# One unit of chunked linear attention: three tiled TensorE stretches put into one, headed by the key transposes, with ScalarE's order refitted

## The chip, the cores and the metric

The kernel is one program on one core of a Trainium2 chip. The metric is the device time of one execution in microseconds. Engines are called PE (TensorE), DVE (VectorE), ACT (ScalarE), POOL (GpSimd) and SP (SyncE, which issues the DMAs).

## The reference, cut to what matters

A small hybrid model on 2 x 1024 tokens of 256 features: linear attention with decay (32 heads of 64), an FFN, softmax attention (16 heads of 16), and the FFN again, each behind a layer norm and with a residual. The change touches the linear attention alone:

```python
qkv = silu(h @ qkv_w.T); q, k, v = split(qkv)          # 32 heads of 64
def step(state, blk):                                  # blocks of the sequence
    aw    = einsum("bhid,bhjd->bhij", qi, ki) * dd     # scores with decay mask
    intra = einsum("bhij,bhjd->bhid", aw, vi)
    inter = einsum("bhid,bhde->bhie", qi * qd_, state)
    new   = state * bd_ + einsum("bhsd,bhse->bhde", ki * kd_, vi)
    return new, intra + inter
attn = rmsnorm(attn) * norm_w;  gate = sigmoid(h @ gate_w.T)
x = x + (gate * attn) @ out_w.T
```

## The kernel before, in words

`linear_attention` walks the work in 32 units. A unit is four heads (two pairs, `pr`) on 512 tokens; unit `u` is `unit(i, j)` with `u = 8 i + j`. Four units make one quad of heads (2048 tokens), whose weights (`w_quads`, 1280 KB) SP loads behind the unit with `j % 4 == 3` of the quad before. The sequence is cut into chunks of 64 tokens, eight in a unit.

PE has two kinds of work in a unit. The **dense** kind uses the whole 128x128 array: `project(..., "v")`, `"g"` (gate), `"k"`, `"q"` and `outputs` (the out projection), each in two halves `n` on the PSUM banks `R[0]` and `R[1]`, each half 12 matmuls (of 256 columns for v and the out projection, of 512 for g, k and q). The **tiled** kind uses the array as quarters of 64x64: `carried` (q times the state, 64 matmuls, 56 where the unit starts a sequence), `within` (masked scores times v, 32 for the blocks of one parity, 32 for the other), `scores` (64) and `state_sums` (k times v per chunk, 64). `turned_keys` transposes the keys by 16 transposes of 64 rows x 128 columns.

The order on PE in a unit j before (lines 716 to 766):

- `carried(j)`, `within(j, True)`, first half of `scores(j+2)` (tiled)
- v of j+2 (dense)
- `within(j, False)`, `state_sums(j+1)`, second half of `scores(j+2)` (tiled)
- g of j+1, k of j+3 (dense)
- `turned_keys(j+2)` (64x128 transposes)
- `outputs(j)`, q of j+3 (dense)

Each engine has its own order written out by hand, with semaphores between them. ACT evicts each projection from `R[n]` through an activation (`evict`, `silu_ok`; a projection into `R[n]` waits until its last content is read), rounds y to its high part (`yh`), squares the outputs (`sq`) and writes the transposed keys times their decay (`keys`: four activations, `kd_ok`, which `state_sums` waits for). DVE forms y = gate times output (`gated`), runs the chain of states (`states`), masks the scores (`masks`) and adds the out projection to the sum (`sums`), then splits weights. POOL decays the queries (`decayed`, after `half_ok`), writes the low part of y, adds the squares and writes the low parts of weights. Units 16 to 27 also carry a piece `c` of the FFN's weight quantisation (`quant`) on ACT, DVE, POOL and SP.

In the last two units (`last`, j = 6 and 7) there is no v, k or q left; ahead of unit 30 PE sums the squares (`fin.squares`, 16 matmuls), and ACT takes a square root of them at the head of its unit 30.

Of the kernel before, what the change touches and what calls it, by code (L numbers as in the profile page):

```python
# [167 lines left out]
def linear_attention(nc, ctx, X, ident, ident_in, hTh, hTl, hidden, w_quads, c_quads, ln2, fin, q, WF, w_ffn, q_ffn, small):  # L168

    with ExitStack() as mem:  # L170
# [41 lines left out]
        def step(i, j):  # L212
            return (i + 1, j - 8) if j >= 8 else (i, j)

        def has(last, j, ahead):
            return not (last and j + ahead > 7)
# [10 lines left out]
        def links(i, j):  # L227
            i, j = step(i, j)
            return LINKS[8] * i + LINKS[j + 1]
# [112 lines left out]
        def _(act):  # L342
            def evict(i, j, kind, n, count):
                act.wait_ge(proj_ok, count + 1)
                bank = R[n][:]
                if kind == "v":
                    act.activation(v[:, j % 4, 2 * n:2 * n + 2, :], bank.rearrange("p (t n) -> p t n", t=2),  # L347
                                   ACT.Silu).then_inc(silu_ok, 1)
                elif kind == "g":
                    act.activation(g[:, j % 2, n, :], bank, ACT.Tanh, scale=0.5).then_inc(silu_ok, 1)  # L350
                elif kind == "k":
                    act.activation(k[:, j % 2, n, :], bank, ACT.Silu).then_inc(silu_ok, 1)
                else:
                    act.activation(q[:, j % 4, n, :], bank, ACT.Silu).then_inc(silu_ok, 1)  # L354
# [13 lines left out]
            def unit(i, j, last, c=None):  # L368
                n0 = evicted(i, j, last)
                if last and j == 6:  # L370
                    act.wait_ge(init_ok, 4)
                    act.wait_ge(fin.ss_ok, 1)
                    act.activation(fin.std[:, 0:4], SC[0][:, 0:4], ACT.Sqrt, bias=fin.epst[:],
                                   scale=4.0 / FEAT).then_inc(fin.std_ok, 1)
                zh, _ = high_low(last, j)
                if has(last, j, 2):
                    for n in range(2):
                        evict(*step(i, j + 2), "v", n, n0 + n)
                    n0 = n0 + 2
                for pr in range(2):  # L380
                    act.wait_ge(y_ok, 16 * i + 2 * j + pr + 1)
                    act.activation(zh[:, pr, :], y[:, pr, :], ACT.Copy).then_inc(yh_ok, 1)  # L382
                if last and j == 7:
                    ln2["scaled"](act, 0, hbuf)
                for pr in range(2):
                    act.wait_ge(sqa_ok, 16 * i + 2 * j + pr + 1)
                    act.activation(sq[:, pr, :], O[pr][:], ACT.Square).then_inc(sq_ok, 1)
                    if has(last, j, 1) and not (last and j == 6):
                        evict(*step(i, j + 1), "g", pr, n0 + pr)
                if last and j == 6:  # L390
                    for pr in range(2):
                        evict(i, 7, "g", pr, n0 + pr)
                if has(last, j, 1):
                    n0 = n0 + 2
                if has(last, j, 3):
                    for n in range(2):
                        evict(*step(i, j + 3), "k", n, n0 + n)
                if has(last, j, 2):
                    for pr in range(2):
                        keys(*step(i, j + 2), pr)  # L400
                if c is not None:
                    quant.rounding(act, c)
                if has(last, j, 3):
                    for n in range(2):
                        evict(*step(i, j + 3), "q", n, n0 + 2 + n)
                if c is not None:
                    quant.overflow(act, c)
                if last and j == 6:
                    act.activation(fin.std[:, 4:8], SC[0][:, 4:8], ACT.Sqrt, bias=fin.epst[:],
                                   scale=4.0 / FEAT).then_inc(fin.std_ok, 1)  # L410
                    ln2["deviation"](act, 0)
                if last and j == 7:
                    ln2["high"](act, 0, banks=SC)
# [39 lines left out]
            for n in range(2):  # L453
                evict(0, 0, "g", n, 12 + n)
            for pr in range(2):
                keys(0, 1, pr)
                evict(0, 2, "k", pr, 14 + pr)
            for n in range(2):
                evict(0, 2, "q", n, 16 + n)
# [132 lines left out]
        def _(pe):  # L592
# [49 lines left out]
                                             k[half[h], j % 2, pr, c * P:(c + 1) * P], ident[half[h], half[h]])  # L642
                m.then_inc(kb_ok, 1)

            def scores(j, pairs=range(2)):
                for pr in pairs:
                    for c in range(GC):
                        for h in range(2):
                            for par in range(2):
                                tok = slice((2 * c + par) * CH, (2 * c + par + 1) * CH)  # L650
                                at = (pr * GC + c) * CH
                                m = pe.matmul(SC[h][half[par], at:at + CH], k[half[h], j % 2, pr, tok],
                                              q[half[h], j % 4, pr, tok], start=True, stop=True)
                if 1 in pairs:
                    m.then_inc(sc_ok, 1)

            def state_sums(j):
                for pr in range(2):
# [10 lines left out]
            def carried(j):  # L669
                n0 = 1 if j % 2 == 0 else 0  # L670
                for n in range(n0, 2 * GC):
                    tok = slice(n * CH, (n + 1) * CH)
                    at = 8 * (j % 2) + n - 1
                    for pr in range(2):
                        for h in range(2):
                            pe.matmul(O[pr][half[h ^ pr], tok], S[half[h], at, pr, :], qd[half[h], pr, tok],
                                      start=n == n0, stop=False, skip_group_check=True)
# [38 lines left out]
            def unit(i, j, last):  # L716
                n0 = evicted(i, j, last)
                pe.wait_ge(mask_ok, 16 * i + 2 * j + 2)
                pe.wait_ge(s_link, links(i, j))
                pe.wait_ge(qd_ok, 16 * i + 2 * j + 2)  # L720
                pe.wait_ge(sq_ok, 16 * i + 2 * j + 1)
                carried(j)
                within(j, True).then_inc(half_ok, 1)
                if has(last, j, 2):
                    pe.wait_ge(silu_ok, n0 - 1)
                    pe.wait_ge(mask_ok, 16 * i + 2 * j + 4)
                    scores((j + 2) % 8, (0,))
                if has(last, j, 2):
                    for n in range(2):
                        pe.wait_ge(silu_ok, n0 + n - 1)  # L730
                        project(*step(i, j + 2), "v", n)
                    n0 = n0 + 2
                pe.wait_ge(half_ok, 8 * i + j + 1)
                within(j, False).then_inc(o_ok, 1)
                if last and j == 7:
                    outputs(i, 6, last, evicted(i, 6, last) + 2)
                    pe.wait_ge(mask_ok, 8 * NQ)
                    pe.wait_ge(fin.std_ok, 2)
                    ln2["turn"](pe, 0, H=hbuf, banks=SC)
                if has(last, j, 1):  # L740
                    pe.wait_ge(kd_ok, 32 * i + 4 * j + 8)
                    state_sums((j + 1) % 8)
                if has(last, j, 2):
                    scores((j + 2) % 8, (1,))
                if has(last, j, 1):
                    for n in range(2):
                        if has(last, j, 2):
                            pe.wait_ge(silu_ok, n0 + n - 1)
                        else:
                            pe.wait_ge(acc_ok, 16 * i + 2 * j + n)  # L750
                        project(*step(i, j + 1), "g", n)
                    n0 = n0 + 2
                if has(last, j, 3):
                    for n in range(2):
                        pe.wait_ge(silu_ok, n0 + n - 1)
                        project(*step(i, j + 3), "k", n)
                    n0 = n0 + 2
                if has(last, j, 2):
                    pe.wait_ge(s_link, links(i, j + 1))
                    turned_keys((j + 2) % 8)  # L760
                if not (last and j == 6):
                    outputs(i, j, last, n0)
                if has(last, j, 3):
                    for n in range(2):
                        pe.wait_ge(acc_ok, 16 * i + 2 * j + n + 2)
                        project(*step(i, j + 3), "q", n)
# [30 lines left out]
            for n in range(2):  # L797
                pe.wait_ge(silu_ok, 11 + n)
                project(0, 0, "g", n)
            pe.wait_ge(s_link, links(0, 0))  # L800
            turned_keys(1)
            for n in range(4):
                pe.wait_ge(silu_ok, 13 + n)
                project(0, 2, "kq"[n // 2], n % 2)
# [1294 lines left out]
```

## Time and profile before

| | |
|---|---|
| median of 3 runs | 1116.5 us (1115.07 to 1119.46) |
| profiled execution, its own time | 1122.47 us |
| span of the profiled execution | 1120.7 us |
| PE busy | 1074.7 us (96%) |
| DVE, ACT, POOL busy | 594.9, 620.4, 495.6 us |
| linear attention loop, first to last unit | from 50.9 to about 640 us |
| one unit | 19.25 us, 19.15 where it starts a sequence |

In the timeline a row is a group of like instructions: start, time from the first start to the last end, engine, line, what is written and read, how many; in square brackets the idle time before it. Matmuls overlap, so two rows that follow each other overlap too; the time a matmul takes from the next is the distance of their starts. In `--windows` rows there follow PE, PE's weight loads, DVE, ACT and POOL busy with their counts, the granted clock as a share, and the DMA share.

### The profile page before, as it was taken

Reading aid. Unit: us, or ns where it says so; the run is one execution under the profiler, and the core shown is the slowest. Engines: PE = TensorE matmul, PEld = TensorE weight load, DVE = VectorE, ACT = ScalarE, POOL = GpSimd, SP = SyncE. Lnnn points to the kernel's source line nnn. Section 1 sums busy time; section 2 is a strip of 40 time slices with the busy share of each in tenths; the row PEclk is TensorE's granted clock in tenths of the full one; section 3 lists DMA queues with packets and bytes.
Section 4 is the critical chain, followed back from the end, with each engine's and each line's share of the span. In section 5 each row is a group of like instructions: output and inputs, shape, how many; then the busy total and the mean of one; then the engine's idle time right before and its main releaser. Section 6 shows DMA issues by size and latency. Waiting matters only on the chain. (4 is left out here: it accounts for less than half of the span.)

```text
span 1120.7 us, 33656 instructions
## 1 busy us (share of the span) xinstructions
PE 1074.7 (96%) x14448; PEld 832.7 (74%) x14448; DVE 594.9 (53%) x1341; ACT 620.4 (55%) x1172; POOL 495.6 (44%) x528
## 2 busy tenths in 40 slices
PE   4999999999999999999999899978899999999998
PEld 4888888888888888888888788856444444445787
DVE  6143434333343545454453755587777778775433
ACT  4553444444443555555554575585477777766663
POOL 2354445354454555554644537644233332221346
PEclk9999999999999999999999989988999999999999
DMA  3100101001001002002004110057523233000001
GB/s 132 56 3 3 56 3 50 9 3 49 17 2 49 25 23 77 24 16 84 17 23 155 35 53 1 18 123 173 100 58 58 58 58 59 2 3 1 1 20 57
DMA packets 19296, 49.15 MB, mean 44 GB/s; under 512 B 2576, under 2 KB 13648, under 8 KB 16464
## 3 DMA queue, kind: packets, MB, share of 16 engines
q1 hardware_dynamic: 19152, 47.04, 15.4%
q8 instruction: 114, 1.87, 0.7%
q14 instruction: 30, 0.25, 0.1%
HBM read 36.08 MB, written 10.75 MB: 42 GB/s over the span
## 5 line engine op out<-in xcount | busy, mean ns | idle before, releaser
L1884 DVE TENSOR_REDUCE aa_mx<-aa_S 128x1 f32<-128x640 f32 (+1 forms) x192 | 174.3, 953 | 54.5 <-PE aa_S L1597 52.6
L506 DVE SCALAR_TENSOR_TENSOR la_y<-la_g,la_O 128x512 f32<-128x512 f32 x64 | 41.1, 683 | 222.5 <-PE la_O L686 222.5
L1789 ACT ACTIVATE aa_PT<-keep 128x512 f32<-128x512 f32 (+1 forms) x204 | 111.6, 580 | 47.1 <-PE keep L1623 45.0
L596 PE MATMUL la_R<-a_hTh,WF 128*128 128x512 f32 x384 | 130.2, 404 | 4.4 <-DVE a_hTl L153 4.4
L1508 POOL TENSOR_SCALAR_AFFINE_SELECT aa_PT<-aa_PT 128x256 f32<-128x256 f32 (+1 forms) x112 | 49.2, 440 | 184.4 <-ACT aa_PT L1789 181.1
L304 POOL TENSOR_TENSOR la_yl<-la_y,la_yh 128x512 fp32r<-128x512 f32 x62 | 79.1, 1299 | 90.2 <-ACT la_yh L382 90.2
L291 POOL TENSOR_TENSOR la_qd<-q,la_C 128x512 f32<-128x512 f32 x64 | 80.8, 1284 | 80.0 <-PE la_O L686 79.7
L513 DVE TENSOR_TENSOR X<-la_R,X 128x512 f32<-128x512 f32 x64 | 44.2, 691 | 118.4 <-PE la_R L596 118.3
L1594 PE MATMUL aa_S<-aa_stacks 96*128 96x512 bf16 (+3 forms) x384 | 99.1, 331 | 4.4 <-DVE aa_mx L1884 3.9
L347 ACT ACTIVATE la_v<-la_R 128x512 f32<-128x512 f32 x64 | 38.2, 598 | 113.5 <-PE la_R L596 113.5
L1069 POOL TENSOR_TENSOR f_fl<-f_f,f_fh 128x512 fp32r<-128x512 f32 x48 | 61.8, 1296 | 66.4 <-ACT f_fh L932 66.4
L354 ACT ACTIVATE q<-la_R 128x512 f32<-128x512 f32 x64 | 38.3, 598 | 93.6 <-PE la_R L596 93.6
L312 POOL TENSOR_TENSOR fin_sqacc<-fin_sqacc,la_sq 128x512 f32<-128x512 f32 x64 | 86.1, 1346 | 7.7 <-DVE X L1191 3.1
L596 PEld LDWEIGHTS la_R<-a_hTh,WF 128*128 128x128 f32 x384 | 72.8, 190 | 22.1 <-DVE a_hTl L153 4.8
L495 DVE SCALAR_TENSOR_TENSOR la_S<-la_S,la_C,la_Y 128x64 f32<-128x64 f32 x448 | 88.6, 273 | 0.2
L596 PE MATMUL la_R<-a_hTh,la_Wh 128*128 128x512 f32 x192 | 77.6, 404 | 0.0
L596 PE MATMUL la_R<-a_hTl,WF 128*128 128x512 f32 x192 | 76.2, 397 | 0.0
L596 PE MATMUL la_R<-a_hTh,la_Wl 128*128 128x512 f32 x192 | 75.9, 396 | 0.0
L596 PE MATMUL la_R<-a_hTl,la_Wh 128*128 128x512 f32 x192 | 75.8, 395 | 0.0
L1623 PE MATMUL keep<-aa_stacks 99*128 99x512 bf16 (+3 forms) x260 | 72.0, 326 | 2.3 <-DMA aa_stacks<-aa_MXT 0.8
L1789 ACT ACTIVATE aa_PT<-aa_ST 128x512 f32<-128x512 f32 (+1 forms) x100 | 58.3, 583 | 25.4 <-PE aa_ST L1623 24.4
L1639 PE MATMUL aa_OB<-aa_PT,aa_V 128*32 128x512 f32 (+3 forms) x768 | 71.7, 492 | 0.0
(306 smaller groups left out, 2804.3 us busy)
## 6 DMA issues: line engine op xcount, KB each, us to landing
la_Wraw<-w_quads_dram SPq DMA_DIRECT2D x7, 1280.0 KB, 6.8
aa_stacks<-k_parts SPq DMA_DIRECT2D x16, 256.0 KB, 6.8
q_parts<-aa_QP SPq DMA_DIRECT2D x8, 384.0 KB, 4.7
aa_stacks<-q_parts SPq DMA_DIRECT2D x8, 384.0 KB, 4.6
k_parts<-aa_KP SPq DMA_DIRECT2D x8, 384.0 KB, 4.9
qw_w<-w_ffn_dram SPq DMA_DIRECT2D x12, 192.0 KB, 2.4
q_ffn<-qw_w SPq DMA_DIRECT2D x12, 192.0 KB, 1.9
X<-hidden_dram SPq DMA_DIRECT2D x4, 512.0 KB, 7.3
```

The source lines that it names most:

```text
L291: pool.tensor_tensor(qd[:, pr, :].rearrange("p (c t) -> p c t", t=CH), q[:, j % 4, pr, :].rearrange("p (c t) -> p c t", t=CH), C[:, slot, ...
L304: pool.tensor_tensor(zl[:, pr, :], y[:, pr, :], zh[:, pr, :].bitcast(F32), ALU.subtract).then_inc(yl_ok, 1)
L312: pool.tensor_tensor(sqacc[:, tok], sqacc[:, tok], sq[:, pr, :], ALU.add).then_inc(sqa_ok, 1)
L495: ins = dve.scalar_tensor_tensor(S[:, at, pr, :], S[:, at - 1, pr, :], C[:, slot, C_B + pr:C_B + pr + 1], U, ALU.mult, ALU.add)
L596: m = pe.matmul(out, a, b, start=n == 0, stop=n == len(pairs) - 1)
L1069: pool.tensor_tensor(fl[:, tb % 2, it, :], f[:, n % FR, :], fh[:, tb % 2, it, :].bitcast(F32), ALU.subtract).then_inc(fl_ok, 1)
L1508: pool.affine_select(part, part, [[0, max(nh, 2)], [1, P]], ALU.is_ge, 0.0, base=0, channel_multiplier=-1).then_inc(cut_ok, 1)
L1594: ins = pe.matmul(bank[:, col:col + k1 - k0], Q[0:SROWS, j, qt * P:(qt + 1) * P], K[0:SROWS, j, k0:k1], start=True, stop=True)
L1623: ins = pe.matmul(ST[at % NB][:, e * w:(e + 1) * w], KS[g % NSL][0:KROWS, h + e, kt * P:(kt + 1) * P], QS[g % NSL][0:KROWS, h + e, q0:q0 + ...
L1639: ins = pe.matmul(OB[32 * j:32 * j + 32, q0 - qb * TB:q0 - qb * TB + w], V[:, 8 * (g // NG) + kt, HG * (g % NG) + j, :], PT[:, (NM2 * g + ...
L1789: act.activation(PT[:, (NM2 * g + b) % NPT, h:h + nh, 0:w], ST[at % NB][:, 0:nh * w].rearrange("p (h q) -> p h q", h=nh), ACT.Exp, scale=S ...
L1884: dve.reduce_max(out, src, AXX).then_inc(s1_free, 1)
```

## The change

PE's order in a unit becomes: `turned_keys(j+1)`, `carried(j)`, `within(j, True)`, all of `scores(j+2)`, `within(j, False)`, `state_sums(j+1)`; then the dense v (j+2), g (j+1), k (j+3), `outputs(j)`, q (j+3). The transposes are made for the keys of j+1 at the head of unit j, where before they were made for j+2 at its end; the prologue's transposes of unit 1 go with them. ACT writes the keys of j+1 first in its unit, then yh, then the squares each followed by an eviction of v, then g, k, q. The other engines' programs are as before.

```diff
 # ACT
-                if has(last, j, 2):
-                    for n in range(2):
-                        evict(*step(i, j + 2), "v", n, n0 + n)
-                    n0 = n0 + 2
+                if has(last, j, 1):
+                    for pr in range(2):
+                        keys(*step(i, j + 1), pr)
                 for pr in range(2):
                     act.wait_ge(y_ok, 16 * i + 2 * j + pr + 1)
                     act.activation(zh[:, pr, :], y[:, pr, :], ACT.Copy).then_inc(yh_ok, 1)
+                values = 2 if has(last, j, 2) else 0
...
                     act.activation(sq[:, pr, :], O[pr][:], ACT.Square).then_inc(sq_ok, 1)
-                    if has(last, j, 1) and not (last and j == 6):
+                    if values:
+                        evict(*step(i, j + 2), "v", pr, n0 + pr)
+                n0 = n0 + values
+                if has(last, j, 1) and not (last and j == 6):
+                    for pr in range(2):
                         evict(*step(i, j + 1), "g", pr, n0 + pr)
...
-                if has(last, j, 2):
-                    for pr in range(2):
-                        keys(*step(i, j + 2), pr)
...
             for pr in range(2):
-                keys(0, 1, pr)
                 evict(0, 2, "k", pr, 14 + pr)
 # PE
+                if has(last, j, 1):
+                    turned_keys((j + 1) % 8)
                 carried(j)
                 within(j, True).then_inc(half_ok, 1)
                 if has(last, j, 2):
-                    pe.wait_ge(silu_ok, n0 - 1)
+                    pe.wait_ge(silu_ok, n0)
                     pe.wait_ge(mask_ok, 16 * i + 2 * j + 4)
-                    scores((j + 2) % 8, (0,))
-                if has(last, j, 2):
-                    for n in range(2):
-                        pe.wait_ge(silu_ok, n0 + n - 1)
-                        project(*step(i, j + 2), "v", n)
-                    n0 = n0 + 2
+                    scores((j + 2) % 8)
                 pe.wait_ge(half_ok, 8 * i + j + 1)
                 within(j, False).then_inc(o_ok, 1)
...
                     state_sums((j + 1) % 8)
                 if has(last, j, 2):
-                    scores((j + 2) % 8, (1,))
+                    for n in range(2):
+                        pe.wait_ge(silu_ok, n0 + n - 1)
+                        project(*step(i, j + 2), "v", n)
+                    n0 = n0 + 2
...
-                if has(last, j, 2):
-                    pe.wait_ge(s_link, links(i, j + 1))
-                    turned_keys((j + 2) % 8)
                 if not (last and j == 6):
                     outputs(i, j, last, n0)
...
-            pe.wait_ge(s_link, links(0, 0))
-            turned_keys(1)
```

## Rows read from the trace of the kernel before

**Rows 1.** The page: busy time, share of the span and instructions of PE.
```profile
PE 1074.7 (96%) x14448; PEld 832.7 (74%) x14448; DVE 594.9 (53%) x1341; ACT 620.4 (55%) x1172; POOL 495.6 (44%) x528
```

**Rows 2.** Busy time of the engines in two whole units, 13 and 14.
```profile
319.72:338.87 19.15, 19.15 (x350) 16.62 (x349) 7.50 (x23) 8.56 (x16) 9.61 (x8) 1.00 0.01 2
300.47:319.72 19.25, 19.25 (x358) 16.72 (x357) 7.48 (x24) 8.55 (x16) 10.28 (x9) 1.00 0.01 3
```

**Rows 3.** Timeline of PE in unit 13, around the projection of v.
```profile
301.45 0.65 PE L686 MATMUL la_O<-la_A,la_v 64*64 64x64 f32 x32
301.92 0.65 PE L652 MATMUL la_SC<-q,la_k 64*64 64x64 f32 x32
302.50 0.39 PE L596 MATMUL la_R<-la_Wh,a_hTh 128*128 128x256 f32 x1
302.72 0.28 PE L596 MATMUL la_R<-la_Wl,a_hTh 128*128 128x256 f32 x1
...
305.30 0.28 PE L596 MATMUL la_R<-la_Wh,a_hTl 128*128 128x256 f32 x1
305.51 0.69 PE L686 MATMUL la_O<-la_A,la_v 64*64 64x64 f32 x32
306.02 1.11 PE L663 MATMUL la_Y<-la_v,la_kd 64*64 64x64 f32 x64
```

**Rows 4.** Timeline of PE in unit 13, around the transposes; one row cuts them at eight.
```profile
312.77 0.39 PE L596 MATMUL la_R<-a_hTl,WF 128*128 128x512 f32 x1
313.00 0.40 PE L596 MATMUL la_R<-a_hTh,WF 128*128 128x512 f32 x1
313.33 0.71 PE L641 MATMUL la_Y<-ident,la_k 64*128 64x64 f32 x16
...
313.33 0.47 PE L641 MATMUL la_Y<-ident,la_k 64*128 64x64 f32 x8
...
313.98 0.38 PE L596 MATMUL la_R<-la_Wh,la_yh 128*128 128x256 f32 x1
314.20 0.29 PE L596 MATMUL la_R<-la_Wl,la_yh 128*128 128x256 f32 x1
```

**Rows 5.** Timeline of DVE in unit 13: y.
```profile
306.37 1.28 DVE L506 SCALAR_TENSOR_TENSOR la_y<-la_g,la_O 128x512 f32<-128x512 f32 x2 [7.30 <-PE la_O L686]
```

**Rows 6.** Timeline of ACT in unit 13 and at the head of unit 14.
```profile
307.09 1.23 ACT L382 ACTIVATE la_yh<-la_y 128x512 fp32r<-128x512 f32 x2 [0.88 <-DVE la_y L506]
308.22 0.58 ACT L387 ACTIVATE la_sq<-la_O 128x512 f32<-128x512 f32 x1
...
312.04 0.60 ACT L352 ACTIVATE la_k<-la_R 128x512 f32<-128x512 f32 x1 [0.80 <-PE la_R L596]
...
314.08 1.57 ACT L365 ACTIVATE la_kd<-la_Y,la_C 128x256 f32<-128x256 f32 x4
...
319.83 0.60 ACT L354 ACTIVATE q<-la_R 128x512 f32<-128x512 f32 x1 [0.80 <-PE la_R L596]
```

**Rows 7.** Timeline of POOL in unit 13: the decayed queries.
```profile
302.21 2.52 POOL L291 TENSOR_TENSOR la_qd<-q,la_C 128x512 f32<-128x512 f32 x2 [0.70 <-PE la_O L686]
```

**Rows 8.** Timeline of ACT at the head of unit 18, a unit with quantisation.
```profile
397.51 0.52 ACT L1159 ACTIVATE qw_k<-qw_w 128x384 f32<-128x384 f32 x1
```

**Rows 9.** Timelines of PE and of ACT at units 30 and 31.
```profile
623.43 1.04 PE L676 MATMUL la_O<-la_qd,la_S 64*64 64x64 f32 x56
...
629.86 1.16 PE L676 MATMUL la_O<-la_qd,la_S 64*64 64x64 f32 x64 [0.21 <-issue]
...
623.58 1.28 ACT L373 ACT_TABLE_LOAD   x1 [3.09 <-PE la_SC L1180]
```

**Rows 10.** Unit 15: PE's scores, SP's weight load; the page's row of instruction loads.
```profile
345.35 1.06 PE L652 MATMUL la_SC<-q,la_k 64*64 64x64 f32 x32
...
344.70 0.33 SPq L253 DMA_DIRECT2D la_Wraw<-w_quads_dram  x1
...
q8 instruction: 114, 1.87, 0.7%
```

More of the change, by code:

```diff
@@ L643, in turned_keys, with scores @@
                 m.then_inc(kb_ok, 1)
-            def scores(j, pairs=range(2)):
-                for pr in pairs:
+            def scores(j):
+                for pr in range(2):
                     for c in range(GC):
@@ L653, in scores @@
                                               q[half[h], j % 4, pr, tok], start=True, stop=True)
-                if 1 in pairs:
-                    m.then_inc(sc_ok, 1)
+                m.then_inc(sc_ok, 1)
             def state_sums(j):
```

## The prediction

> **What bounds the kernel now.** I read the page's busy times first, then the engines' busy time in windows of whole units, then the timeline of PE instruction by instruction, and last the timelines of ACT, DVE and POOL beside it. PE is busy 96% of the span [rows 1], and in a unit of the linear attention it is never idle: 19.15 of 19.15 us and 19.25 of 19.25 us, at a granted clock of 1.00, which is the level of 2.4 GHz [rows 2]. The other engines are busy 7.5 to 10.3 us of the 19 in the same windows. So in this stage, some 590 of 1120.7 us, nothing but the time from one matmul's start to the next's counts, and a wait would have to be new to matter. Busy, though, hides something: a busy PE is not a PE at its pitch. The timeline shows it at each change between whole-array matmuls and tiled ones. A dense matmul of 256 columns starts (305.30 - 302.72) / 22 = 0.117 us after the one before, one of 512 columns 0.23 us (313.00 - 312.77), and 32 tiled matmuls of an undisturbed run take 0.47 us (301.45 to 301.92) [rows 3, 4]. At the changes the steps are longer, and the change is about those.
>
> **The change part by part.** No instruction is added or removed, on any engine. PE's matmuls of a unit are the same in number and shape. What changes is how often PE passes between dense and tiled: three rounds (into tiled and back) in a unit before, one after.
>
> *The round around v goes.* From the rows [rows 3]: the 32 scores ahead of v take 0.58 us until the first dense matmul, 0.11 over 0.47. The first dense one takes 0.22 until the second, 0.10 over 0.117. The last dense one takes 0.21 until `within`, 0.09 over 0.117. The first 32 tiled ones behind it take 0.51, 0.04 over 0.47. Sum 0.34 us. It goes in the 30 units that have a projection of v: 10.2 us.
>
> *The round around the transposes goes.* The last dense matmul takes 0.33 us until the transposes, 0.10 over 0.23. The eighth transpose ends 0.47 us after the first's start, the sixteenth 0.71 [rows 4]: the last four pairs take 0.24 us, 0.06 a pair, where the first three steps take 0.25 for 0.18, so 0.06 over. (With the 0.22 us that one lasts, the last pair starts at 313.82.) From there to the dense one at 313.98 it is 0.16, 0.10 over a pair, and that first dense one takes 0.22, 0.10 over. Sum about 0.35; I take 0.34. It goes in 30 units and once in the prologue: 31 x 0.34 = 10.5 us.
>
> *A new junction comes.* The transposes (64 rows x 128 columns) now stand straight ahead of `carried` (64x64), 31 times. No row of before shows these two side by side. Below: `within`, `state_sums` and `scores` follow each other at the usual pitch though they differ in operands and banks, so 0; nothing in it could make it a gain. Above: as much as a whole round, 0.34. I take 0.15, the nearest rows' price for leaving one array shape (0.10 to 0.11) and for the first group in the new one (0.04 to 0.06), without the 0.10 that only the full-width first weights cost. 31 x 0.15 = 4.7 us. The rule that bears on it is in the Trainium skill, "TensorEngine Tiling (Array Packing)", Key Properties: a change of the tiling mode drains the array, a change of the tile does not. The trace agrees where it can: 64x64 work on other quarters of the array flows at pitch, and each of six mode changes costs. By that rule 64x128 to 64x64 is a change of mode and is paid, against this change; by the reading that both count as tiled the sum would be 4.7 us better.
>
> *Waits, one by one, with T the start of a unit's transposes.* The times follow from the pitches above: transposes to T+0.55, junction, `carried` T+0.7 to 1.6, `within` to 2.1, `scores` to 3.05, `within` to 3.5, `state_sums` to 4.45, then v0 from 4.6, v1 6.05, g0 7.45, then one half each 1.4 us, `outputs` from 13.1, q to 18.65.
> (a) `state_sums` waits for the keys, which before were written half a unit early. ACT first finishes the last eviction of q, 0.11 to 0.71 us into the unit by where it lies before (319.83 against 319.72) [rows 6]. The transposes are out at T+0.75, the four key activations take 1.57 us [rows 6], so they end at T+2.4, with the 0.52 us of quantisation ahead of them [rows 8] at T+2.7. PE wants them at T+3.5: 0.8 us of slack. Behind the keys on ACT stands yh, which can't start before T+4.6 anyway.
> (b) `scores` now waits for both halves of q, evicted at T+0.7; wanted at T+2.1.
> (c) g0 waits for the eviction of v0, which now stands behind yh and a square. y starts 0.35 us after the last `within` matmul is issued (306.37) [rows 5] or so, T+3.9; yh0 0.72 us later, the square 1.13 after that (307.09, 308.22), so it runs from T+5.75 to 6.3 [rows 6]. v0's last matmul ends at T+6.25. The eviction thus runs at T+6.3 to 6.9, and g0 wants the bank at T+7.45: 0.5 us of slack, as much as k has behind g before, where ACT idles 0.80 us ahead of an eviction [rows 6] and PE does not wait. Behind it: the second square, v1, g0, each ahead of its need.
> (d) POOL's decayed queries start at T+2.3 in place of T+1.7 and take 2.52 us [rows 7]; wanted at T+18.65. The wait of `within(j, False)` for the first half is covered by the scores between them. `outputs` and `sums` keep their distance to the unit's end, so POOL's, DVE's and SP's later work does too. The state chain follows y at T+5.2 and has the whole dense stretch.
>
> *The end.* In unit 30 ACT has a table load of 1.28 us [rows 9] and a root (0.3 allowed) ahead of the keys, so they end 0.15 + 1.28 + 0.3 + 1.57 = 3.3 us after the squares; PE would reach `state_sums` after 2.8. Behind the sums the chain of states on DVE releases unit 31. Before it starts 6.43 us behind unit 30 (629.86 against 623.43) [rows 9], just about when the states are ready; I find 7.35 from the transposes on where the transposes and junction alone give 7.1. Loss 0.3 us.
>
> *Sum.* -10.2 - 10.5 + 4.7 + 0.3 = -15.7 us. A unit goes from 19.25 to 18.7 us. The span goes from 1120.7 to 1105.0 and the profiled execution's own time from 1122.5 to 1106.8. The median of the runs shown is 6.0 under that execution, so 1116.5 - 15.7 = 1100.8.
>
> **The rivals.**
> *A. PE's instructions don't keep up.* The longest tiled run now is 16 + 64 + 64 + 64 + 64 = 272 matmuls with as many weight loads, before it was 128. The instruction queue loaded 114 blocks, 1.87 MB, so 16 KB each [rows 10], and PE's 2 x 14448 instructions [rows 1] over 114 make 253 a block. A tiled run eats a block in 127 x 0.0146 = 1.9 us, and one long run now eats two. For it: in unit 15 the 32 scores at the very end of a run took 1.06 us in place of 0.65 [rows 10], 0.4 us lost, in the stretch that SP's weight load began at 344.70. Against: it is one of 30 units. If each long run lost that 0.4, the gain would be 15.7 - 12 = 4 us: 1113. In a sentence for itself: the Trainium skill, "Runtime: NRT & Kernel Launch", Instruction fetch mechanics, gives PE room for 2048 instructions in blocks of 256, by which a run of 544 would never wait; no run here shows that room.
> *B. The same, with the weights in the way (slower than before).* SP starts a load of 1280 KB in seven units at `o_ok`, now T+3.9, with `state_sums` and v behind it. If PE then stood until its next block came through behind that load, it would wait up to the load's length, some 5 us: 7 x 5 = 35, less 15.7, gives 1136. It makes the kernel slower from 2.2 us a load on. Against: v and g eat only some 70 instructions in their 2.8 us, and in unit 15 it cost 0.4.
> *C. ACT is late for v.* If y, yh and square came 1.1 us later than reckoned, PE would stand 0.6 us ahead of g0 in 30 units: the gain is spent, 1117. From 0.5 us of lateness on it costs something. Nothing ahead of y on DVE is in its way: it idled 7.30 us there [rows 5].
> *D. The junction costs a whole round.* Then 31 x 0.19 more: 1107.
>
> **How the numbers follow.** My forecast (with a junction anywhere from 0 to D) has 0.80: 1096 to 1107. A 0.09, B 0.04, C 0.07. The range that should hold it 8 times in 10 reaches from the junction at 0 to a little past D, towards A: 1095 to 1110. A measurement here tells 0.5%, 5.6 us, from no change. Faster by more: the 0.80 and half of A and a little of C, 0.86. Within: the rest of A and most of C, 0.09. Slower: B and the tail of C, 0.05.
>
> **What would show it.** A unit of 18.7 us (18.6 at a sequence's start) with PE busy throughout; two dense-to-tiled steps fewer; behind the transposes a first step of `carried` between 0.06 and 0.4 us, which is the junction; no row of PE waiting for ACT's keys or for v's eviction; ACT's idle time ahead of v0's eviction near 0. Wrong would be a unit above 19.0, a step over 0.3 us inside a tiled run (A, B), or a gap ahead of g0 (C).

## The result, and the profile after

The changed kernel takes 1142.1 us (median of 4 runs, 1141.32 to 1145.1) where the kernel before takes 1116.3 beside it: a ratio of 1.021, 95% interval 1.018 to 1.024, so 25.8 us slower by the medians where 15.7 us faster was forecast. (A slip ahead of the prediction: a half of g, k or q is 6 matmuls of 512 columns, not 12; the durations used there, 1.4 us a half, are those of 6.)

The busy times of the page, to be read against [rows 1], and the waits of PE in the whole span (line waited at, releaser, us in all, times, longest):

```profile
PE 1060.5 (93%) x14445; PEld 830.8 (73%) x14448; DVE 591.1 (52%) x1341; ACT 619.7 (54%) x1172; POOL 493.5 (43%) x528
```

```profile
PE la_Y L662 <- issue: 19.3, 15, 1.7
...
PE la_O L685 <- issue: 8.2, 8, 1.5
...
PE la_SC L652 <- issue: 3.7, 5, 1.4
...
PE la_R L596 <- issue: 1.7, 3, 0.7
...
PE la_Y L662 <- ACT la_kd L365: 0.3, 1, 0.3
```

"issue" is idle time for which no semaphore and no DMA of the program can be named. There are 31 such waits, 32.9 us in all, where the loop before had next to none; one wait of 0.3 us is for ACT's keys. Two whole units (13 and 14), and the loop from the first `carried` to the last one's start, before and after (after the window: PE, PE's weight loads, DVE, ACT, POOL busy, granted clock, DMA share, GB/s):

```profile
310.90:331.37 20.47, 19.03 (x360) 16.83 (x357) 7.57 (x24) 8.56 (x17) 10.23 (x9) 1.00 0.01 2
331.37:351.54 20.17, 18.88 (x352) 16.71 (x349) 7.59 (x23) 8.56 (x17) 9.27 (x8) 1.00 0.01 2
51.31:655.70 604.39, 571.07 (x10753) 505.50 (x10749) 242.19 (x725) 279.70 (x537) 289.00 (x224) 1.00 0.10 33
```

```profile
50.94:629.86 578.92, 578.47 (x10749) 502.72 (x10749) 245.69 (x725) 279.52 (x532) 291.22 (x224) 1.00 0.10 34
```

The units answer to [rows 2]: 20.5 and 20.2 us for 19.25 and 19.15. The loop took 25.5 us more, at the same granted clock of 1.00 and with 7 us less of PE busy: the whole difference of the medians is here. (The profiled spans differ by 19.6 only, since the profile of before had the lower clock level, 1.2 GHz, for longer behind this loop: the mean granted clock over the span is 0.989 against 0.997.)

PE's timeline in unit 13, then in unit 12 and unit 14 (start, time, what, how many; in brackets the idle time before):

```profile
309.93 0.39 PE L596 MATMUL la_R<-a_hTh,la_Wl 128*128 128x512 f32 x1
310.25 0.72 PE L641 MATMUL la_Y<-ident,la_k 64*128 64x64 f32 x16
310.90 1.16 PE L675 MATMUL la_O<-la_qd,la_S 64*64 64x64 f32 x64
311.88 0.65 PE L685 MATMUL la_O<-la_A,la_v 64*64 64x64 f32 x32
312.35 1.11 PE L652 MATMUL la_SC<-q,la_k 64*64 64x64 f32 x64
313.28 0.65 PE L685 MATMUL la_O<-la_A,la_v 64*64 64x64 f32 x32
313.75 0.64 PE L662 MATMUL la_Y<-la_v,la_kd 64*64 64x64 f32 x28
315.83 0.80 PE L662 MATMUL la_Y<-la_v,la_kd 64*64 64x64 f32 x36 [1.44 <-issue]
...
293.86 0.28 PE L662 MATMUL la_Y<-la_v,la_kd 64*64 64x64 f32 x2
295.03 1.15 PE L662 MATMUL la_Y<-la_v,la_kd 64*64 64x64 f32 x62 [0.89 <-issue]
...
334.10 1.11 PE L662 MATMUL la_Y<-la_v,la_kd 64*64 64x64 f32 x61
336.50 0.27 PE L662 MATMUL la_Y<-la_v,la_kd 64*64 64x64 f32 x2 [1.29 <-issue]
```

PE stops in the middle of `state_sums`, where the code has no wait at all: behind its 2nd, its 28th and its 61st matmul in units 12, 13 and 14. Count the instructions, a weight load and a matmul for each product. In unit 12 the stop comes 2 x (56 + 32 + 64 + 32 + 2) = 372 instructions behind the start of `carried`, in unit 13 it is 2 x (64 + 32 + 64 + 32 + 28) = 440, and unit 12 has 700 instructions: 700 - 372 + 440 = 768, three times 256. Unit 13 has 717, the stop in unit 14 is at 2 x (56 + 32 + 64 + 32 + 61) = 490, and one more since the weight load of the next product had run ahead of it: 717 - 440 + 491 = 768. PE's instructions were seen to come in blocks of about 256 [rows 10], and each of the 31 stops (28 inside a tiled run, 3 within the first dense matmuls behind one) lies at the same count modulo 256, weight loads, matmuls and waits counted. So did the 0.4 us stop of unit 15 before, and so do all 135 stops inside or just behind a tiled run in the loops of the seven kernels below.

The answer to [rows 6] and [rows 5], ACT's and DVE's timelines in unit 13:

```profile
311.01 1.57 ACT L365 ACTIVATE la_kd<-la_Y,la_C 128x256 f32<-128x256 f32 x4
314.83 1.23 ACT L381 ACTIVATE la_yh<-la_y 128x512 fp32r<-128x512 f32 x2 [2.25 <-DVE la_y L506]
315.96 0.58 ACT L387 ACTIVATE la_sq<-la_O 128x512 f32<-128x512 f32 x1
318.27 0.60 ACT L347 ACTIVATE la_v<-la_R 128x512 f32<-128x512 f32 x1 [1.74 <-PE la_R L596]
```

```profile
314.11 1.28 DVE L506 SCALAR_TENSOR_TENSOR la_y<-la_g,la_O 128x512 f32<-128x512 f32 x2 [5.26 <-PE la_O L685]
```

The keys end at 312.58, 1.2 us ahead of `state_sums` at 313.75, and ACT idles 1.74 us ahead of v's eviction: neither is late. (That idle time, forecast as near 0, is PE's stop passed on.)

### The profile page after: what moved, and what is told of

Same layout as the page of the kernel before. It is cut to its first block and busy times, and to the rows that moved or that the text cites. A ratio compares the mean times of both kernels' runs of the same rounds, so it can differ in the third digit from the quotient of the medians.

```text
span 1140.3 us, 33653 instructions
## 1 busy us (share of the span) xinstructions
PE 1060.5 (93%) x14445; PEld 830.8 (73%) x14448; DVE 591.1 (52%) x1341; ACT 619.7 (54%) x1172; POOL 493.5 (43%) x528
## 5 line engine op out<-in xcount | busy, mean ns | idle before, releaser
L381 ACT ACTIVATE la_yh<-la_y 128x512 fp32r<-128x512 f32 x62 | 38.1, 632 | 77.2 <-DVE la_y L506 77.2
L1783 ACT ACTIVATE aa_PT<-aa_ST 128x512 f32<-128x512 f32 (+1 forms) x100 | 58.3, 583 | 25.8 <-PE aa_ST L1617 24.8
```

Of the source, the lines that this page charges most:

```text
L1783: act.activation(PT[:, (NM2 * g + b) % NPT, h:h + nh, 0:w], ST[at % NB][:, 0:nh * w].rearrange("p (h q) -> p h q", h=nh), ACT.Exp, scale=S ...
```

## The experiments

Three theories were set against each other.

**I, supply.** PE's instructions come in blocks of 256, and the next block is asked for when PE enters the last one loaded. A block needs some 3.6 us from there until it can be used; 256 instructions of tiled work are gone in 1.9 us. Two block boundaries inside one tiled run make PE stand; dense work alone, 15 us a block and more (128 matmuls at 0.117 or 0.233 us), never does. **II, keys.** PE waits for ACT, whose keys are now late. **III, length.** PE issues tiled work more slowly than it runs it, whatever the addresses: about 9 ns for each matmul beyond 128 in a run.

All times below are ratios to the kernel before in the same comparison. The forecast of stalls under I went through the order of a unit with a block boundary each 256 instructions, 64 instructions of lead for PE's queue and a block time of 3.6 to 3.7 us; lead and block time were fitted to the 28 stops above.

**e1_turn_head**: the kernel before, with only the transposes (and ACT's keys) at the unit's head, and those of the prologue gone with them.

```diff
+                if has(last, j, 1):
+                    turned_keys((j + 1) % 8)
                 carried(j)
...
-                if has(last, j, 2):
-                    pe.wait_ge(s_link, links(i, j + 1))
-                    turned_keys((j + 2) % 8)
 # ACT: keys(j + 1) first in the unit, keys(j + 2) gone; v, yh, squares as before
```

> Only the transposes are moved to the unit's head (keys first on ACT); v stays in the middle, scores stay split. Tiled runs of 144 and 128 matmuls (288 and 256 instructions). Theory I (PE's instructions come in blocks of 256 and the next block is not there when two block boundaries fall within one tiled run, 1.9 us apart; a block takes about 3.6 us from boundary to use): two boundaries hardly ever fit, one stall at most; one round of 0.34 less, a junction of 0.14 more, -6 us against before. Theory II (PE waits for ACT's keys, which now come late): state_sums stands 7 us behind the transposes here, no wait, -6 us too. Theory III (PE issues tiled work slower than it runs it, so each tiled matmul beyond some 128 in a run costs 9 ns): 16 beyond, 0.15 us a unit, -1 us.

Measured 0.994 (0.992 to 0.997), 1109.9 against 1119.0 us by the medians, 6.4 us less by the ratio. Theories I and II had -6, III -1. Its PE waits only twice for instructions inside the loop:

```profile
PE la_SC L651 <- issue: 0.5, 2, 0.3
```

**e2_v_join**: the changed kernel with the transposes back at the end, behind k, and the keys of j+2 half a unit early, as before.

```diff
-                if has(last, j, 1):
-                    turned_keys((j + 1) % 8)
                 carried(j)
...
+                if has(last, j, 2):
+                    pe.wait_ge(s_link, links(i, j + 1))
+                    turned_keys((j + 2) % 8)
                 if not (last and j == 6):
                     outputs(i, j, last, n0)
 # ACT: keys as before, the rest as changed
```

> Only v is moved out of the tiled work (as in the changed kernel, with ACT's order for v); the transposes stay at the unit's end with the keys half a unit early, as before. One tiled run of 256 matmuls (512 instructions). Theory I: two boundaries nearly always fall into the run, some 27 stalls of 1.3 us, 35 us, less 10 for the round saved: +24 us. Theory II: the keys are early, no wait, one round less: -10 us. Theory III: 128 matmuls beyond, 1.15 us a unit, +25 us.

Measured 1.028 (1.024 to 1.031), 31 us more. With early keys PE stops as it did; theory II, at -10, has fallen; I (24) and III (25) can't be told apart by it. The stops (PE's waits):

```profile
PE la_Y L663 <- issue: 17.8, 15, 1.6
...
PE la_O L686 <- issue: 8.1, 8, 1.3
...
PE la_R L597 <- issue: 2.1, 2, 1.1
PE la_SC L653 <- issue: 1.1, 1, 1.1
```

**e3_v_mid** and **e4_v_late**: the changed kernel with v ahead of `within(j, False)`, and ahead of `state_sums`.

```diff
                     scores((j + 2) % 8)
+                    for n in range(2):                        # e3
+                        project(*step(i, j + 2), "v", n)
                 within(j, False).then_inc(o_ok, 1)
+                    for n in range(2):                        # e4
+                        project(*step(i, j + 2), "v", n)
                     state_sums((j + 1) % 8)
 # ACT in e3: v evicted ahead of yh, as before; in e4 as changed
```

> The changed kernel with v between the scores and the second within; transposes at the head. Tiled runs of 176 and 96 matmuls (352 and 192 instructions). Theory I: two boundaries fit into the first run only where the first falls into its first 90 instructions or so, and only half of those are close enough: about 7 stalls, 5 us in all, with -6 for the round: -1 us. Theory II: -6 us. Theory III: 48 beyond, 0.43 us a unit, +7 us.

> The changed kernel with v between the second within and state_sums. Tiled runs of 208 and 64 matmuls (416 and 128 instructions). Theory I: about 15 stalls, 16 us in all, with -6 for the round: +9 us. Theory II: the keys have 2.8 us more than in the changed kernel: no wait, -6 us. Theory III: 80 beyond, 0.72 us a unit, +16 us.

Measured 1.002 (1.000 to 1.004), 2 us more, for e3, and 1.011 (1.007 to 1.015), 12 us more, for e4. The longest tiled run is 128, 144, 176, 208, 256 and 272 matmuls in before, e1, e3, e4, e2 and the changed kernel, and the cost goes 0, -6, +2, +12, +31, +26: more or less with the length. What parts theory I from III is how it is paid: in e3 by whole stops in 8 of 30 units (5 in the scores, 3 just behind them), and the other 22 run without any: 19.03 and 18.95 us as in e1, but for two of 19.1.

```profile
PE la_SC L652 <- issue: 4.3, 5, 1.1
PE la_R L596 <- issue: 2.4, 3, 1.4
```

III would have put 0.43 us into every unit, +7, outside e3's interval (0 to 4 us). In e4 both I (9) and III (16) lie within the interval of 8 to 17. Of I's numbers e2 and e4 came out above (31 for 24, 12 for 9), e3 too (2 for -1). For e3 the trace says why: it has 8 stops, 6.7 us idle and 0.26 us more for each (worked out below), where 7 of 5 us in all were expected.

**p1_shift_a** and **p2_shift_b**: addresses alone. In the order of e3, a dense matmul of 512 columns can be issued as two of 256. From unit 2 on both kernels split the same ones, so many that a unit is 768 instructions, three blocks, give or take one; units 0 and 1 differ, and with them the place in a unit at which the block boundaries stand. In both, the sums in the banks of split projections are not those of the reference; the instructions and their order are as told.

```diff
-            SPLITS = [0, 0, 33, 25, 34, 25, 33, 25, 34, 25, ...]       # p1
+            SPLITS = [30, 6, 33, 25, 34, 25, 33, 25, 34, 25, ...]      # p2
```

> The order of e3_v_mid with some of the 36 dense matmuls of 512 columns of a unit issued as two of 256 columns each (same columns, same products, 2 instructions more for each), 25 to 34 of them from unit 2 on, so that each unit is 768 instructions, three blocks, and the block boundaries stay at one place of the unit from then on. Here none is split in units 0 and 1, which puts a boundary some 67 instructions behind the start of the transposes, and so the next one 256 on, still in the first tiled run. Theory I: a stall of about 1 us in each of some 30 units, +24 us against before. Theory III (cost by the length of the run, whatever the addresses): as e3_v_mid, +2. A theory by which it is the array's own work or another engine that holds PE: as e3_v_mid, +2.

> The same as p1_shift_a, and the same splits from unit 2 on; only units 0 and 1 have 30 and 6 matmuls split, which moves the boundaries by 72 instructions, to some 251 behind the start of the transposes, so that only one falls into the first tiled run. Theory I: no stall at all from then on, -6 us against before, 30 under p1_shift_a. Theory III and any that doesn't go by instruction addresses: as p1_shift_a.

Measured 1.031 (1.027 to 1.035) for p1 and 1.005 (1.002 to 1.007) for p2: 35 and 5 us over before. PE's waits in p1, then in p2:

```profile
PE la_SC L660 <- issue: 21.6, 22, 2.7
...
PE la_R L596 <- issue: 4.4, 6, 1.2
```

```profile
PE la_SC L660 <- issue: 3.1, 3, 1.6
```

The two kernels do the same work in the same order from unit 2 on, and differ by 29 us (30 expected), because the one has its boundaries 67 and 323 instructions behind the transposes' start and the other at 251. A theory that knows nothing of instruction addresses gives no difference here. Both are some 10 us above what I expected. About 6 us of it is the splitting's own price: two halves take 0.240 us where a whole matmul takes 0.233, and the units of p2 without a stop last 0.2 us longer than those of e3. In p1 the 29 stops took 26.3 us idle, and 0.26 us more each makes 34 of the 35 us measured, since the splitting's 6 us and the order's gain of 6 cancel. In p2 the rest is its three stops, 3.1 us idle, where none was expected. The boundaries creep on by 20 instructions from unit 2 to 29, so that in p2 from unit 6 on one stands at the very start of the run and the next fits into it too; the stops are in units 20, 24 and 29. Two units of p2, 11 and 12, to be read against 19.03 and 18.95 in e3:

```profile
263.14:282.37 19.23, 19.23 (x385) 18.12 (x382) 6.82 (x22) 8.44 (x17) 7.61 (x6) 1.00 0.19 71
282.37:301.54 19.17, 19.17 (x386) 18.46 (x382) 7.15 (x21) 8.46 (x17) 9.65 (x7) 1.00 0.08 23
```

**d1_scores3**: the block time by itself.

```diff
-                    scores((j + 2) % 8)
+                    for n in range(3):
+                        scores((j + 2) % 8, n == 2)
```

> The changed kernel with the scores of a unit computed three times over in place (128 more tiled matmuls, 256 more instructions in the one tiled run of 30 units; the result is that of the last). At the pitch of tiled matmuls they cost 1.87 us a unit, 56 us. Theory I: a run then holds one more block boundary than before the addition, and each boundary behind the first comes a whole block time, 3.6 us, after the last: 2 stalls a unit, +111 us against the changed kernel; the distance from the end of one stall to the end of the next is the block time itself. Theory III (9 ns for each tiled matmul beyond 128 in a run): 3.0 us a unit, +90 us, with no boundary to be seen. PE held by another engine (Theory II): only the pitch, +56 us.

Measured 1256.8 us (median of 2 runs), ratio 1.124 (1.115 to 1.133): 115 us above the changed kernel, 111 expected under I, 90 under III and 56 under II. PE's timeline in unit 9, in which two stops follow each other inside one run:

```profile
268.44 2.16 PE L652 MATMUL la_SC<-q,la_k 64*64 64x64 f32 x133
271.71 1.09 PE L652 MATMUL la_SC<-q,la_k 64*64 64x64 f32 x58 [1.11 <-issue]
...
275.44 0.68 PE L663 MATMUL la_Y<-la_v,la_kd 64*64 64x64 f32 x27 [1.64 <-issue]
```

From the end of one stop to the end of the next it is 3.73 us (271.71 to 275.44). Over the 27 pairs of stops 256 instructions apart (in 26 units) it is 3.45 to 4.02 us, 3.72 in the mean. In the pair shown PE goes on at 271.71, the queue's next load runs from 272.80 to 274.00, and PE goes on from its next stop at 275.44. That is the block time with no lead and no queue in it: 14.5 ns an instruction, 29 ns a tiled product, where the array itself takes 14.6.

## Why the prediction was wrong

*The two rounds.* Right. Units without a stop show it: e1, which saves one round and pays the junction, has units of 19.03 and 18.95 us for 19.25 and 19.15 before [rows 2], 0.2 less for 0.34 - 0.14 = 0.20. Its gain of 6.4 us (interval 3.5 to 9.4) fits 31 x 0.20 = 6.2.

```profile
298.96:317.99 19.03, 19.03 (x360) 16.78 (x356) 7.48 (x24) 8.56 (x17) 10.27 (x9) 1.00 0.01 3
317.99:336.94 18.95, 18.95 (x352) 16.70 (x349) 7.51 (x23) 8.57 (x17) 9.32 (x8) 1.00 0.01 2
```

No run isolates v's round, but units 13 and 14 of the changed kernel, less what their stops cost (1.44 and 1.29 us idle and 0.26 each, below), come to 18.8 and 18.6 us where 18.7 and 18.6 were forecast.

*The junction.* Predicted 0.15 us. Measured 0.14: in the instruction records from the last pair of transposes to `carried` it is 0.153 us for 0.06 a pair, and the first group of four takes 0.048 more than the next. The rule of the Trainium skill, "TensorEngine Tiling (Array Packing)", Key Properties, that a change of tiling mode drains the array, agrees with this: the change from 64x128 to 64x64 is paid too.

*The waits on ACT, DVE and POOL.* Right, (a) to (d): y at T + 3.86 us for 3.9 (314.11 against 310.25), the square at T + 5.7 for 5.75, the keys 1.2 us early, POOL's queries at T + 2.4 for 2.3. ScalarE's new order cost nothing; the single 0.3 us on the keys is the one foreseen in unit 30.

*Instructions come for nothing.* This is the step that failed. The sum had no term for them. Rival A, which named the very mechanism, priced it at 0.4 us a run by the one stop of unit 15 [rows 10] and gave it a chance of 0.09. Measured, every one of the 30 units had a stop, and a stop cost 1.3 us in the mean. But the stop of unit 15 was the edge of the effect: a run of 256 instructions, which just held two boundaries. Before, no tiled run was longer than that, and the kernel sat right at the limit. A run of 544 instructions holds two boundaries always, 1.9 us apart, and pays the block time less 1.9 us and less the fitted lead of the queue: 3.7 - 1.9 - 0.5 = 1.3 us. The 31 stops took 32.9 us idle. Each cost 0.26 us more in time that still counts as busy, mostly the last matmul ahead of it and a slower first group behind it (from 16 matmuls ahead of a stop to 12 behind it, against the usual pitch, mean of 24 stops): 8.0 us. With -20.7 for the rounds and +4.4 for the junctions that is +24.6, of 25.5 measured in the loop; some 1 us I can't place.

The numbers to see it were there: tiled work eats a block in 1.9 us [rows 3, 10], and 114 block loads were in the profile. What was missing was the block's time from request to use, which no row of before showed, and an unknown with a price of 1 us in each of 30 units should have been bounded from both sides as the junction was. In its place stood the Trainium skill's figure for PE's room, "Runtime: NRT & Kernel Launch", Instruction fetch mechanics: 2048 instructions in blocks of 256. The trace does not agree: with such room a run of 544 could not starve behind a dense stretch of 14 us, and it starves in each of 30 units. In unit 13 the queue's loads run from 305.25 to 306.53 and from 313.20 to 314.59, with none between, and PE stops for want of the second at 314.39. PE behaves as with two blocks of 256, the one it works in and the next, which is what the same section of the Trainium skill says of the other engines. Rival B leaned on a slip too: v and g are the 72 instructions told there, but they last 5.7 us, not 2.8. Its load of weights was not needed for any of it; the longest stop of p1, 2.7 us, fell beside large loads in units 29 to 30, and whether these stretch a block's time was not tried.

**A version that beats both** is e1_turn_head, 0.994 (0.992 to 0.997) of before: the transposes moved, v left where it was, runs of 288 and 256 instructions. By the same account, which no run tests here, one round cannot be had: all tiled work of a unit is 544 instructions, and a run without a stop must hold no second boundary, so under 512 with the boundary placed by hand.

## What to carry to other kernels

Count instructions, not only time: a stretch of small matmuls has a length limit in instructions, here 256 and a little more, beyond which PE waits for its own program, and dense work between such stretches is what pays for them. Merging stretches to save mode changes (0.34 us a round here) is worth it up to that length only. An idle time put down to "issue", inside a run that has no wait in the code and always at the same count modulo 256, is the sign of it.

## What the runs showed of the hardware

- PE's instructions arrive in blocks of 256 (16 KB); from one block to the next 3.45 to 4.02 us where nothing else holds PE, mean 3.72 (27 pairs in d1). Of that the load itself is 0.9 to 1.4 us, and PE goes on 1.2 to 1.6 us after the load's end (the 31 stops of the changed kernel).
- In dense work alone a block lasts 15 to 30 us (128 matmuls at 0.117 or 0.233 us), so nothing is seen; at the 14.6 ns of a 64x64 product PE could use one each 1.9 us.
- A dense matmul of 512 columns issued as two of 256 takes 0.240 us in place of 0.233 (p2).
- The time of a kernel can hang on where its instructions lie: p1 and p2 differ by 29 us through 72 instructions more in the first two units.
